# All four chunks of keys ahead of the units of values in the full-array phase of a two-layer cross-attention kernel

## The reference, cut to what matters

```python
qn = layernorm(x, ln_q_g, ln_q_b)
q = qn @ Wq * scale
k, v = jnp.split(media @ Wkv, 2, axis=-1)          # 16 heads of 64 each
sim = jnp.einsum('bhid,bhjd->bhij', q, k)
sim = jnp.where(media_mask[:, None, None, :], sim, neg_inf)
out = jnp.einsum('bhij,bhjd->bhid', softmax(sim), v)
x = x + tanh(attn_gate) * (out @ Wo)
...
```

## Time and profile before

| | |
|---|---|
| median of 3 runs (lowest, highest) | 932.42 us (931.53, 936.5) |
| the profiled execution: its time, its span | 932.89 us, 931.1 us |
| PE busy | 857.9 us, 92% of the span |
| DVE, ACT, POOL busy | 66%, 47%, 42% |

### The profile page before, as it was taken

How to read it: one execution, slowest core, us unless ns; L and a number is a source line. 1 busy time by engine, 2 the same in 40 slices (tenths; PEclk the granted TensorE clock), 3 DMA queues, 4 the chain that set the end, 5 groups by cost and what they waited for, 6 DMA issues and landing times.

```text
span 931.1 us, 18175 instructions
## 1 busy us (share of the span) xinstructions
PE 857.9 (92%) x7811; PEld 716.2 (77%) x7811; DVE 616.2 (66%) x945; ACT 440.5 (47%) x665; POOL 392.3 (42%) x179
## 2 busy tenths in 40 slices
PE   3589999999999999999999999999998899979887
PEld 2488787788888878878887788888886688768675
DVE  5766788978848898694688978746878321043453
ACT  2255545555625556553555555535565331143342
POOL 0035555555635656565355555545566610000000
PEclk9689999999999999999999999999999999989999
DMA  7100001000000010000000000000006000001100
GB/s 254 32 1 2 1 1 36 2 1 2 1 2 1 1 37 1 2 1 2 1 2 1 2 1 2 1 1 1 2 2 196 2 1 1 1 0 42 42 12 23
DMA packets 19697, 16.67 MB, mean 18 GB/s; under 512 B 913, under 2 KB 18722, under 8 KB 19490
## 3 DMA queue, kind: packets, MB, share of 16 engines
q1 hardware_dynamic: 19618, 15.51, 5.4%
HBM read 14.46 MB, written 1.05 MB: 17 GB/s over the span
## 4 chain that ended last, share of the span: by engine, by line
PE 76%; DVE 14%; ACT 4%; issue 2%; POOL 1%; DMA 1%; SPq 0%; POOLq 0%; DVEq 0%
PE psum L1061 21%; PE psum L1075 15%; PE psum L315 13%; PE psum L1032 6%; PE psum L998 3%; PE psum L927 3%; PE psum L1097 3%; PE psum L939 3%; PE psum L1166 2%; DVE mx L779 2%; DVE k_lo L772 2%; PE psum L1087 1%; DVE negl L788 1%; ACT v L513 1%; POOL acc L412 1%
## 5 line engine op out<-in xcount | busy, mean ns | idle before, releaser
L412 POOL TENSOR_TENSOR acc<-acc,ring 128x1024 f32<-128x1024 f32 x128 | 306.2, 2392 | 18.9 <-POOL acc L412 0.4
L779 DVE TENSOR_REDUCE mx<-psum 128x2 f32<-128x800 f32 (+2 forms) x256 | 245.2, 989 | 84.9 <-PE psum L1032 78.4
L528 ACT ACTIVATE ring<-psum 128x1024 f32<-128x1024 f32 x192 | 197.1, 1027 | 72.4 <-PE psum L1061 65.9
L407 POOL TENSOR_TENSOR acc<-ring 128x1024 f32<-128x1024 f32 x32 | 76.7, 2395 | 325.3 <-ACT ring L528 325.3
L1075 PE MATMUL psum<-ring,v 128*64 128x256 f32 (+1 forms) x1664 | 186.7, 381 | 1.7
L1075 PEld LDWEIGHTS psum<-ring,v 128*64 128x64 f32 (+1 forms) x1664 | 116.7, 137 | 60.6 <-DVE k_lo L772 3.8
L1061 PE MATMUL psum<-nm,maskrow 64*128 64x256 f32 (+1 forms) x832 | 126.1, 298 | 1.7 <-DVE maskrow L761 1.6
L1061 PE MATMUL psum<-q_lo,k_hi 64*128 64x256 f32 (+1 forms) x832 | 119.2, 281 | 0.0
L1061 PE MATMUL psum<-q_hi,k_lo 64*128 64x256 f32 (+1 forms) x832 | 118.7, 279 | 0.0
L1061 PE MATMUL psum<-q_hi,k_hi 64*128 64x256 f32 (+1 forms) x832 | 118.5, 279 | 0.0
L1032 PE MATMUL psum<-k_hi,q_hi 64*128 64x400 f32 (+1 forms) x512 | 96.8, 375 | 8.9 <-DVE mx L779 4.1
(11 more groups left out here) (149 smaller groups left out, 1367.1 us busy)
## 6 DMA issues: line engine op xcount, KB each, us to landing
nat<-in_ctx_dram SPq DMA_DIRECT2D x8, 768.0 KB
w<-in_L_xattn_W_dram SPq DMA_DIRECT2D x2, 1024.0 KB, 8.5
xs<-in_x_dram SPq DMA_DIRECT2D x4, 256.0 KB, 5.3
ring<-in_L_xattn_Wkv_dram SPq DMA_DIRECT2D x1, 1024.0 KB, 7.1
wq<-in_L_xattn_Wq_dram SPq DMA_DIRECT2D x1, 1024.0 KB, 9.2
wo<-in_L_xattn_Wo_dram SPq DMA_DIRECT2D x1, 1024.0 KB, 10.1
out_dram<-t_res SPq DMA_DIRECT2D x8, 128.0 KB, 1.8
mask<-in_mask_BxS_bk_dram SPq DMA_DIRECT2D x4, 200.1 KB, 5.8
```

The source lines that it names most:

```text
L407: nc.gpsimd.tensor_tensor(acc[:, :, :, :], ring[:, 0, :, :, :], ring[:, 1, :, :, :], ALU.add)\
L412: nc.gpsimd.tensor_tensor(acc[:, :, :, :], acc[:, :, :, :], ring[:, g, :, :, :], ALU.add)\
L528: nc.scalar.activation(ring[:, g, :, :, :], score_set[m % 2].rearrange("p (h i q) -> p h i q", h=2, i=2), ACT.Exp).then_inc(S["p_ready"], 1)
L779: nc.vector.tensor_reduce(mx[:, t, :, c], aux_pair[BANK[item] // 2][:, :, 0:min(c1, KEYS) - c0], axis=AX.X, op=ALU.max).then_inc(S["m_max" ...
```

## The change

In `full_phase` the four groups K, L, E come first, then F, then the three or four units of values, then R. Nothing is added or removed.

```diff
     for c in range(4):
         out += [("K", j + 2, c), ("L", j + 2, c), ("E", j - 1, c)]
-        if c < len(units):
-            out.append(("V", n, units[c]))
-    return out + [("F", j - 1), ("R", j + 1)]
+    return out + [("F", j - 1)] + [("V", n, u) for u in units] + [("R", j + 1)]
```

## The result

The changed kernel takes 945.69 us in the median of four runs (942.8 to 948.59), the kernel before 931.97 us beside it (930.01 to 936.5). The ratio is 1.014, with a 95% interval of 1.0087 to 1.0194: slower, by some 14 us. The profiled execution took 942.8 us, with a span of 941.0 us, 9.9 us more than before. The forecast was 951.5 us, within 942 to 959.

A forecast was written before the change was run, and what follows sets the result against it. The prediction took PE to be the bound, held to DVE's pace in full-array phases after the change: 20.4 us lost less 1.4 given back, 19.0 on 932.9, gives 951.9, said as 951.5 us; eight in ten for 942 to 959.

The forecast's parts named there:

- DVE's pace holds PE: Full-array phases: each V waits for an L, and L's follow at 0.95 us against 0.70 us of a V.
- Rivals 1 and 2: 1: PE's loss hidden elsewhere, half 942 (0.08), all 933 to 935 us (0.05); 2: no V waits, faster, 927 us (0.03).
- Its size: PE's loss from first L to first A, summed over the phases with K's: 20.4 us.
- 3 x 0.95 + 0.57 = 3.42 us from first to end of last L: Time DVE needs for the four L's of a full-array phase, at 0.95 us from L to L.
- Rival 3: DVE slower than 0.95 us from L to L, at the sum of durations, 1.11 us: 965 us; chance 0.06.
- The gift behind j=4: Row phase behind j=4: DVE some 1 us earlier, about 0.45 us comes back, three times: 1.4 us.
- The lottery: negl on DVE held up by POOL's additions: one phase more or fewer is worth up to 2.2 us; 4 us either way.
- I expect the same phases to be hit: The phases whose negl POOL holds up stay the same, since all is timed from the row phase's start.
- a count that moves by more than two: Sign of a wrong prediction: the number of long negl, forecast at about eight, moves by more than two.
- Its working out of eight from the mean: Held negl from their 763 ns mean and 2.47 us: ten of 32 if free ones took nothing, eight at a quarter microsecond.
- The start: List ahead of the loop: three phases without E, V's not held; 0.2 us for the one with a stall already.
- Rival 4: PE's clock falls in the new gaps of full-array phases: +80 us if in every phase, 960 in a tenth; chance 0.03.

The follow-up runs named there:

- e1: The changed kernel, with the four reciprocals (E) behind the four L in every full-array phase: 926.79 us, ratio 0.9965 to the kernel before.
- e7: The changed kernel with negl on ACT, and each reciprocal done twice: 982.96 us, ratio 1.0553 to the kernel before.
- e8: The kernel before with negl on ACT, and each reciprocal done twice: 936.74 us, ratio 1.0072 to the kernel before.
- e3: The changed kernel, with negl written by ACT instead of DVE: 938.87 us, ratio 1.0105 to the kernel before.
- e2: The kernel before, with negl written by ACT instead of DVE: 926.96 us, ratio 0.9976 to the kernel before.
- e4: The kernel before, with full-array phases ordered K K V V K K V V: 929.4 us, ratio 1.0006 to the kernel before.
- a2: The changed kernel run once more, beside more runs of the kernel before: 943.41 us, ratio 1.0144 to the kernel before.
- e10: e1 and e2 together (new order, reciprocals behind the four L, negl on ACT): 922.55 us, ratio 0.9941 to the kernel before.
- e12: e10 with C and Z ahead of U in the column phase of j=4: 927.91 us, ratio 0.9971 to the kernel before.
- e11: The kernel before with negl on ACT, and the new order at j=7 alone: 928.84 us, ratio 0.9995 to the kernel before.

## Why the prediction was right, and where it was off

**DVE's pace holds PE: right.** Shown by e1 (E out of the way, loss gone), e7 against e8 (more E, loss grows by 3 x 0.41 us in every phase of the new order, by a small part of that in the old), and by the 0.06 us from end of L to start of V and R in the profile after. Rivals 1 and 2 fell: the loss was not hidden, D comes 5.67 us after the first A in every loop batch, and DVE's distance from L to L stayed above the 0.70 us of a V.

**Its size: 17.7 us for 20.4.** The step was "3 x 0.95 + 0.57 = 3.42 us from first to end of last L". The first distance is 0.95 us, the next two are 0.88, since from the second L on an L is recorded with 0.51 us in place of 0.57 and its E follows after 0.43 us in place of 0.48; the last L thus ends at 3.22 us, not 3.42. The other way went what stands behind the last wait: the first matmul behind a wait is followed after 0.22 us, where others follow at 0.12, so that A comes 0.37 us after R and not 0.27, and a held V takes 0.81 us and not 0.70. So first L to first A became 4.36 and 3.65 us, not 4.45 and 3.75. Rival 3, the sum of durations, fell by the same rows. The trace before did not offer it where the prediction looked: there every L of chunk 2 waits for its `k_hi`, and the pair of the earlier trace rows has the first, longer L in it. Why the later L's are shorter stays open (in e1, with L behind L, they have 0.57 us again).

**The gift behind j=4: right where `negl` is not held, wrong in this comparison.** The forecast was 1.4 us given back; e3 against e2 gives 1.4 us. But in the profiled execution before, `negl` of j=4 was held in all three batches, PE came late to the row phase, and DVE's lateness there showed with 0.5 us only. In the profile after no `negl` of j=4 was held (last S to first L 2.31 us instead of 4.06), PE came early, and the row phase was 0.9 us longer. Timeline of the changed kernel, the place of the earlier trace rows:

```profile
157.15 0.69 DVE L791 TENSOR_TENSOR acc<-acc 128x512 f32<-128x512 f32 x1 [2.26 <-POOL acc L410]
...
162.58 0.73 DVE L720 TENSOR_SCALAR z<-xs,mv,rstd 128x256 f32<-128x256 f32 x2
163.23 4.81 DVE L777 TENSOR_REDUCE mx<-psum 128x2 f32<-128x804 f32 x5
```

The first M there starts at 161.30 us, the first maximum 1.93 us later, against 1.04 in the earlier trace rows. DVE starts U when POOL has ended, and nothing that PE or DVE gains before helps.

**The lottery: its price seen, its stability misjudged.** The step that failed is "I expect the same phases to be hit". Eight were held in the profiled execution before, three after: two that were held before too, and j=8 of batch 0, which was not. The prediction names a count that moves by more than two as a sign of being wrong, and it moved by five; 6.3 us of the difference of the spans hang on it. (Its working out of eight from the mean is loose: it gives 7.4.) `negl` of j=4 came 5.08 us after POOL's first addition in the trace before (151.25 - 146.17) and was held, and 5.05 us after it in the trace after (149.55 - 144.50), and was free. The trace before, then the trace after:

```profile
146.17 2.40 POOL L407 TENSOR_TENSOR acc<-ring 128x1024 f32<-128x1024 f32 x1 [3.90 <-ACT ring L528]
...
151.25 2.43 DVE L788 TENSOR_SCALAR negl<-m 128x128 fp32r<-128x128 f32 x1
...
144.50 2.42 POOL L405 TENSOR_TENSOR acc<-ring 128x1024 f32<-128x1024 f32 x1 [4.37 <-ACT ring L526]
147.06 10.05 POOL L410 TENSOR_TENSOR acc<-acc,ring 128x1024 f32<-128x1024 f32 x4
...
149.55 0.23 DVE L786 TENSOR_SCALAR negl<-m 128x128 fp32r<-128x128 f32 x1
```

It is a matter of who comes first: the held one began 0.02 us behind the start of POOL's third addition (151.22), the free one 0.04 us ahead of it (149.59), in the short gap between two additions. In the loop batches of both traces the free ones lie at 5.01 to 5.06 us and the held ones at 5.08. Why it shifted by these hundredths, and whether the change itself did that, stays open. The Trainium skill, page "SBUF — State Buffer", section "SBUF: two separate sides", gives PE and ACT ports of their own beside the pair that VectorE and GpSimd lock. The runs agree: with `negl` on ACT it took 0.31 us, and no first L was late in any of the 28 phases of e2 or e3.

**The start: left out.** The prediction had 0.2 us for the list ahead of the loop. It looked there at V's waiting for L's alone, and not at what DVE reaches earlier. That won 3 us in this comparison and 4 in e3 against e2, and brings the result to the lower part of the range. It is mostly the clock: e4 has it too, with one of its two waits there as long as before. Rival 4 went the other way in this comparison: the small gaps in the phases left the clock up (mean 0.986 after, 0.98 before), and the one stretch of low clock went. The rival was a real one, though: with the larger gaps of e7 the clock did fall, seven times in the 28 phases. And the digits in the earlier trace rows that spoke against it are coarse: in the trace before the granted clock is 0.79 from 728 to 736 us, and the slice there shows 9.

Put together: 17.7 for 20.4, nothing given back but +2.3, 3.0 won at the start, 6.3 of luck in the profiled execution, and 0.7 at the end. The medians are 13.7 us apart in the first comparison and 12.6 in a2's; how many `negl` were held in the runs behind them is not known, since only one run of each kernel has a trace. That the time lies inside the range thus owes something to terms that cancel.

Runs of one kernel differ by 2 to 12 us. For the kernel before, most of that goes with the granted clock: of the 29 runs beside e1 to e4, the seven at 0.976 or less have a median of 931.6 us, the eight at 0.98 or more 927.2. The same shows in e10: five runs at 0.984 took 922.0 to 922.7 us, three at 0.978 to 0.98 took 926.2 to 926.6. For the eight runs of the changed kernel it does not (943.5 us at 0.98, 948.59 at 0.982), and what spreads those stays open.

## What to carry to other kernels

Where items share a ring of banks, write down for each item which one empties its bank, on which engine, and what that engine does in between; an order costs as soon as the items come faster than the slowest emptier, and moving foreign work from between the emptyings (here the reciprocals) took that cost away in the same order of matmuls. When an instruction comes later than it did, ask first whether the engine stood or ran slower: in e7 the granted clock told that D had waited for nothing. Measure the distance from start to start of back-to-back instructions over the whole run that will be back-to-back afterwards, not a pair. And look at both ends of a reordering: what an engine reaches earlier at the start of the program can pay as much as a stall costs later.

## What was not expected of the hardware

Two waits of PE of 1.06 and 1.62 us, 55 us into the execution, came with some 9 us at a granted clock of 0.65 and 0.58; two of 0.46 us did not (changed kernel, e1, e3, e7, e10 to e12, a2), and neither did 0.67 and 1.66 us in e4. A later wait of 1.42 us (changed kernel, j=8 of batch 0) went by at a granted clock of 1.00. Behind j=4 a wait of 1.80 us came with a fall in e11 and one of 1.78 us in e2 did not. The 2.81 us of D in e12 came with 0.79 in the 6 us around it and 0.93 in the next 6. In e7 no recorded wait in a full-array phase of the 28 was longer than 0.74 us, yet the clock fell behind the one of every j=3 and j=7, and of no other j, though j=5 and 9 have the same waits. So the length of one wait does not tell whether the clock falls; what does is not shown here. And 30 ns in the start of one instruction of DVE decided about 2.2 us.
